# GpSimd computes two of the eight hidden units of every slot of a fused four-layer graph network

## The chip, the cores and the metric

The kernel runs on one core of one Trainium2 chip. The metric is the device time of one execution in microseconds, as the median of a few runs. The work is done by five engines with a program each: TensorE (PE in the profile, with its weight loads as PEld), VectorE (DVE), ScalarE (ACT), GpSimd (POOL) and SyncE (SP), which issues all DMAs here. The engines are tied together by semaphores that the code sets and waits on by hand.

## What is computed

For each of 64 graphs of 128 nodes with 128 features, four layers follow one another, each with a residual and a layer norm. The first is by far the largest:

```python
def _L0_gnn_ref(x, adj, W1, b1, W2, b2, gamma, beta):
    hi = jnp.einsum('bsh,hk->bsk', x, W1[:H])
    hj = jnp.einsum('bsh,hk->bsk', x, W1[H:])
    h = jax.nn.relu(hi[:, :, None, :] + hj[:, None, :, :] + b1)
    y = jnp.einsum('bijk,kl->bijl', h, W2) + b2
    y = _layernorm(y, gamma, beta)
    return jnp.einsum('bij,bijh->bih', adj, y)
...
x = _layernorm(x + _L0_gnn_ref(x, adj, ...), axis=-1)
x = _layernorm(x + _L1_gnn_ref(x, adj, W, b), axis=-1)      # relu((D^-1/2 adj D^-1/2 x) W^T + b)
x = _layernorm(x + _L2_gnn_ref(x, adj, nodemask, ...), axis=-1)   # two-layer perceptron on (1+eps)x + adj^T x
x = _layernorm(x + _L3_gnn_ref(x, adj, ...), axis=-1)      # three rounds of adj^T (h W), norm, relu
```

So for every graph and every node i there is a 128x128 block h_i = relu(v + u_i), where v (hj, turned so that features lie on the partitions) is the same for all i and u_i (hi + b1) is one column. All in float32.

## The kernel before

**Units, slots, graphs.** The 128x128 block of one node i is a unit. Eight units (`DUO_UNITS`) make a slot, in two blocks of four (`BLOCK_UNITS`); a graph has 16 slots (`SLOTS`). Every engine walks through the same sequence of slots s = 0..15 per iteration, and works in slot s on a different stage of an earlier slot t, at a fixed lag (`lagging`). Between its own steps of the first layer each engine has the steps of the three later layers of an older graph ("tails", placed by the table `AT`: slot and one of nine fine places k, `FINE`). In what follows "slot s" is a place in an engine's program, and t the slot of h that is treated there.

**The stages of one slot t.**
- Hidden, lag 4 (`START`): the eight units h = relu(vT + u_i) are made. VectorE makes the first `vector_units(t)` units from vT in SBUF with one tensor_scalar each (L624), two in a slot and four in slot 15: 34 of a graph. ScalarE makes the others, with one activation each that reads v from PSUM (L515, 90 of a graph) or, in slot 15, vT from SBUF (4 of a graph). The `h` buffer holds 16 slots, so that a slot of h can be written only when its weighted sums for the graph before are done (`ttr_done`).
- Products, lag 5: TensorE multiplies each block of four units with W2 into `y_ps` (L377; a float32 product is two instructions in the trace). Block 0 waits for `h_dve` and `h_act_head`, block 1 for `h_act`.
- Squares, lag 6: ScalarE squares the 128x1024 result into `sq` (L525). In its program this stands at the start of each slot, before the hidden units.
- Variances: TensorE sums the squares over the partitions (L389, eight instructions for every two slots). After half a graph ScalarE takes the root (L532), DMAs straighten it, VectorE takes the reciprocal (L646) and multiplies with adj (L654), and DMAs store and spread the coefficients over all partitions (`cb`).
- Weighted sums, lags 18 and 19: VectorE multiplies each unit of h with its row of coefficients and sums (L638, 128 of a graph: a custom instruction that reads h and cb, both in SBUF, and an accumulator read). In slot s it first does units 4 to 7 of one t (fine places 0 to 3), then at place 4 its hidden units, then units 0 to 3 of the next t (places 5 to 8).

At slot 3 TensorE makes u and v of the new graph and ScalarE copies them out (`keep_uv`, L504 and L505, which sets `uv_ready`).

GpSimd has only small steps on 128x1 columns: for each of the seven norms of a graph an addition (L865) and a power -1/2 (L868), and one more power (L860). VectorE needs the power six fine places after the statistics (`NORM_AT`).

The names that the change touches are `vector_units`, ScalarE's `hidden` and the loop that calls it, `keep_uv`, TensorE's `products`, and GpSimd's `iteration`.

Of the kernel before, what the change touches and what calls it, by code (L numbers as in the profile page):

```python
# [12 lines left out]
P = 128  # L13
# [20 lines left out]

NORM_AT = 7
LATER_SET_UP_SLOT = 2


def vector_units(t):

    if t == SLOTS - 1:
        return BLOCK_UNITS
    return 2

# [30 lines left out]
def build(nc, x, adj, nodemask, l0_W1, l0_b1, l0_W2, l0_b2, l0_gamma, l0_beta, l1_W, l1_b,  # L75
# [4 lines left out]
    with ExitStack() as ctx:  # L80
# [6 lines left out]
        def sem(name):  # L87
            return ctx.enter_context(nc.semaphore(name))
# [81 lines left out]
            sem("x_in_in"), sem("x_turned"), sem("xT_set"), sem("uv_made"), sem("uv_ready"))  # L170
        h_dve, h_act_head, h_act = sem("h_dve"), sem("h_act_head"), sem("h_act")
        y_done, sq_done = sem("y_done"), sem("sq_done")
# [178 lines left out]
        def _(pe):  # L351
# [15 lines left out]
            def products(g, t, block_of_duo):  # L367
# [6 lines left out]
                else:  # L374
                    wait(pe, h_act, SLOTS * g + t + 1)
                c0 = block_of_duo * COLS
                op = pe.matmul(y_ps[:, t % 2, c0:c0 + COLS], w2c[:], h[:, t, c0:c0 + COLS], start=True, stop=True)  # L377
# [115 lines left out]
        def _(act):  # L493
# [5 lines left out]
            def keep_uv(g, b):  # L499

                wait(act, uv_made, g + 1)
                wait(act, h_dve, SLOTS * (g - 1))
                wait(act, h_act, SLOTS * (g - 1))
                act.activation(uT[:, b, :], u_ps, ACT.Identity, bias=b1_col[:])  # L504
                act.activation(vT[:, b, :], v_ps, ACT.Copy).then_inc(uv_ready, 1)  # L505

            def hidden(g, b, t, n):
# [8 lines left out]
                if n == BLOCK_UNITS - 1:  # L516
                    op.then_inc(h_act_head, 1)
                if n == DUO_UNITS - 1:
                    op.then_inc(h_act, 1)
# [56 lines left out]
            def iteration(after, graphs, buf):  # L576
                new = graphs[0]
                for s in range(SLOTS):
# [17 lines left out]
                    first = vector_units(ht)  # L596
                    for n in range(first, DUO_UNITS):
                        if n == first + 2:
# [5 lines left out]
                        if hg is not None:  # L604
                            hidden(hg, hb, ht, n)
                    if first == BLOCK_UNITS:
                        tail_steps(6, 8)
# [219 lines left out]
        def _(pool):  # L827
# [26 lines left out]
            def later_layers(g, b, lo, hi):  # L854
# [7 lines left out]
                for name in NORMS:  # L862
                    if lo <= AT[name] + 1 < hi:
# [5 lines left out]
                                           ).then_inc(rs_set[name], 1)  # L869

            pool.wait_ge(ones_set, 5)

            def iteration(after, graphs, buf):
                for s in range(SLOTS):
                    for k in range(FINE):
                        for g, b, place in tails(graphs, buf, s):
                            later_layers(g, b, place + k, place + k + 1)
# [26 lines left out]
```

## Time and profile before

| | us |
|---|---|
| median of three runs (2913.82 to 2915.78) | 2914.24 |
| the profiled execution | 2916.74 |
| its span, first to last instruction | 2915.1 |
| PE busy | 2819.0 (97%) |
| ACT busy | 2824.1 (97%) |
| DVE busy | 2732.0 (94%) |
| POOL busy | 436.3 (15%) |
| mean granted TensorE clock | 0.99 |

Busy time is the time in which at least one instruction of the engine is under way. Instructions of one engine overlap (the next starts before the last has written its result), so the duration of an instruction is not what it costs: that is the distance from its start to the start of the next one when nothing is waited for. Both are used below, and named apart.

### The profile page before, as it was taken

To read this page: it belongs to the slowest core of one execution; us is meant where nothing else is said; L and a number is where in the kernel's file an instruction comes from. 1 tells how busy PE (TensorE), PEld (TensorE's weight loads), DVE (VectorE), ACT (ScalarE), POOL (GpSimd) and SP (SyncE) were. 2 spreads that over 40 slices of the span, in tenths; PEclk is the share of its full clock that TensorE was granted. 3 is DMA by queue.
4 is the path that set the end of the run, shared out by engine and by line. 5 is a ranking of instruction groups with operands and counts; after the bars stand their busy time and mean duration, and the time that the engine had idled before them with its cause. 6 is when DMAs were issued, how large, how long until landed. Compare 5 with 4: busy or idle time off the path is not lost.

```text
span 2915.1 us, 59519 instructions
## 1 busy us (share of the span) xinstructions
PE 2819.0 (97%) x10882; PEld 1093.6 (38%) x10882; DVE 2732.0 (94%) x21521; ACT 2824.1 (97%) x8004; POOL 436.3 (15%) x978
## 2 busy tenths in 40 slices
PE   8999999999999999999999999999999999999994
PEld 2333333333333333333333333333333333333332
DVE  3999999999999999999999999999999999999997
ACT  8999999999999999999999999999999999999992
POOL 0011111111111111111111111111111111111111
PEclk9999999999999999999999999999999999999996
DMA  2544544554555455445545544554554455455442
GB/s 101 225 185 191 223 196 183 212 214 184 194 217 199 185 205 221 185 191 217 203 182 212 213 185 190 221 199 185 208 218 186 185 226 199 183 209 217 185 191 114
DMA packets 170229, 571.63 MB, mean 196 GB/s; under 512 B 68608, under 2 KB 104320, under 8 KB 104320
## 3 DMA queue, kind: packets, MB, share of 16 engines
q1 hardware_dynamic: 169856, 567.82, 49.6%
q14 instruction: 282, 2.31, 0.2%
q8 instruction: 91, 1.49, 0.2%
HBM read 555.17 MB, written 8.39 MB: 193 GB/s over the span
## 4 chain that ended last, share of the span: by engine, by line
ACT 61%; PE 22%; issue 10%; DVE 4%; DMA 2%; SPq 1%; POOL 0%; DVEq 0%; POOLq 0%; ACTq 0%
ACT h L515 36%; ACT sq L525 16%; PE y_ps L377 14%; PE ss_ps L389 4%; ACT dev_rows L532 4%; DVE h L638 2%; ACT xT L497 2%; ACT hid L554 1%; DMA cb<-c_scratch 1%; PE uv_ps L364 1%; PE prod_bank L410 1%; ACT aggT L550 1%; DMA devs<-dev_rows 1%; SPq L294 1%; ACT aggT L558 1%
## 5 line engine op out<-in xcount | busy, mean ns | idle before, releaser
L377 PE MATMUL y_ps<-h,w2c 128*128 128x512 f32 x4096 | 2104.5, 621 | 32.9 <-issue 14.1
L515 ACT ACTIVATE h<-uv_ps,uT 128x128 f32<-128x128 f32 x5760 | 2011.9, 788 | 0.0
L638 DVE CUSTOM_DVE_ANT_0 h<-h,cb 128x128 f32<-128x128 f32 x8192 | 1923.1, 279 | 44.9 <-DMA cb<-c_scratch 42.6
L525 ACT ACTIVATE sq<-y_ps,b2c_col 128x1024 f32<-128x1024 f32 x1024 | 1550.9, 1515 | 24.5 <-PE y_ps L377 24.5
L377 PEld LDWEIGHTS y_ps<-h,w2c 128*128 128x128 f32 x4096 | 647.8, 189 | 1058.4 <-issue 691.6
L638 DVE DVE_READ_ACCUMULATOR2_ANT gT<- 128x1 f32 x8192 | 633.4, 77 | 0.0
L389 PE MATMUL ss_ps<-sq,sel 128*32 128x512 f32 x4096 | 546.4, 605 | 1.1 <-ACT sq L525 1.0
L624 DVE TENSOR_SCALAR h<-vT,uT 128x128 f32<-128x128 f32 x2176 | 501.1, 273 | 6.8 <-ACT mask_all L570 4.8
L865 POOL TENSOR_TENSOR var_eps<-mv,eps_col 128x1 f32<-128x1 f32 x448 | 85.7, 191 | 2004.1 <-DVE mv L665 2004.1
L868 POOL TENSOR_TENSOR rs<-var_eps,minus_half 128x1 f32<-128x1 f32 x448 | 308.5, 689 | 35.0
L389 PEld LDWEIGHTS ss_ps<-sq,sel 128*32 128x32 f32 x4096 | 80.6, 108 | 248.7 <-ACT sq L525 182.7
L646 DVE RECIPROCAL invs<-devs 128x64 f32<-128x64 f32 x128 | 70.6, 552 | 103.6 <-DMA devs<-dev_rows 103.2
L563 ACT ACTIVATE h<-z_aff 128x128 f32<-128x128 f32 x192 | 130.6, 680 | 18.7 <-DVE z_aff L745 18.7
L558 ACT ACTIVATE aggT<-prod_bank 128x128 f32<-128x128 f32 x192 | 128.2, 668 | 20.9 <-PE prod_bank L439 20.9
L515 ACT ACTIVATE h<-vT,uT 128x128 f32<-128x128 f32 x256 | 140.0, 914 | 0.0
L662 DVE BATCH_NORM_STATS2 stats<-z 128x6 f32<-128x128 f32 x448 | 127.0, 283 | 0.3
L532 ACT ACTIVATE dev_rows<-ss_ps 128x512 f32<-128x512 f32 x128 | 116.3, 909 | 1.0 <-PE ss_ps L389 1.0
L443 PEld LDWEIGHTS prod_bank<-l3w,aggT 128*128 128x128 f32 x384 | 68.3, 192 | 126.2 <-ACT aggT L558 89.4
L860 POOL TENSOR_TENSOR dis_raw<-degree_floor,minus_half 128x1 f32<-128x1 f32 x64 | 35.3, 551 | 416.0 <-DVE degree_floor L686 416.0
L443 PE MATMUL prod_bank<-l3w,aggT 128*128 128x128 f32 x384 | 82.7, 298 | 14.4 <-ACT aggT L558 14.2
L671 DVE TENSOR_SCALAR x<-z,mv,rs 128x128 f32<-128x128 f32 x256 | 86.4, 338 | 5.1 <-POOL rs L868 4.8
L665 DVE BATCH_NORM_AGGREGATE mv<-stats 128x2 f32<-128x6 f32 x448 | 76.6, 171 | 0.4
(99 smaller groups left out, 1592.9 us busy)
## 6 DMA issues: line engine op xcount, KB each, us to landing
cb<-c_scratch SPq DMA_DIRECT2D x512, 1024.0 KB, 8.2
adj_c<-in_adj_dram SPq DMA_DIRECT2D x512, 8.0 KB
devs<-dev_rows SPq DMA_DIRECT2D x512, 8.0 KB
x_in<-in_x_dram SPq DMA_DIRECT2D x64, 64.0 KB, 10.6
c_scratch<-c SPq DMA_DIRECT2D x128, 32.0 KB, 1.4
adj_in<-in_adj_dram SPq DMA_DIRECT2D x64, 64.0 KB, 4.3
x_res<-in_x_dram SPq DMA_DIRECT2D x64, 64.0 KB, 5.3
out_dram<-x SPq DMA_DIRECT2D x64, 64.0 KB, 3.0
```

Of the source, the lines that this page charges most:

```text
L377: op = pe.matmul(y_ps[:, t % 2, c0:c0 + COLS], w2c[:], h[:, t, c0:c0 + COLS], start=True, stop=True)
L389: mm = pe.matmul(ss_ps[32 * q:32 * q + 32, :], sel[:, ROWS - 1 - p:ROWS - 1 - p + 32], sq[:, (t + q // 2) % SQ_RING, c0:c0 + COLS], start= ...
L443: pe.matmul(out, aggT[:, b, :], l3w[:, i, :], start=True, stop=False)
L515: op = act.activation(h[:, t, n * P:(n + 1) * P], v, ACT.Relu, bias=uT[:, b, i:i + 1])
L525: act.activation(sq[:, t % SQ_RING, :], y_ps[:, t % 2, :], ACT.Square, bias=b2c_col[:], scale=float(P) ** -0.5).then_inc(sq_done, 1)
L532: act.activation(dev_rows[:, half, :], ss_ps[:], ACT.Sqrt, bias=EPS).then_inc(dev_done, 1)
L558: act.activation(aggT[:, b, :], prod[b], ACT.Copy).then_inc(l3_agg_kept[i], 1)
L563: act.activation(h3[:, b, :], z_aff[:, b, :], ACT.Relu).then_inc(l3_relued[i], 1)
L624: op = dve.tensor_scalar(h[:, t, n * P:(n + 1) * P], vT[:, b, :], uT[:, b, i:i + 1], 0.0, ALU.add, ALU.max)
L638: op = dve.tensor_tensor_reduce(h[:, t, cols], h[:, t, cols], cb[:, t // 2, c0:c0 + P], 1.0, 0.0, ALU.mult, ALU.add, gT[:, i:i + 1])
L662: dve.bn_stats(stats[:, b, :], z[:, b, :]).then_inc(stats_set[name], 1)
L868: pool.tensor_tensor(rs[:, b:b + 1], var_eps[:, b:b + 1], minus_half[:], ALU.pow).then_inc(rs_set[name], 1)
```

## The change

GpSimd gets two of the eight units of every slot, 32 of a graph: the last unit (7), at fine place 0 of the slot in which the other engines make theirs, and the unit before it (6), at fine place 6 of the slot ahead of that. It makes them from vT and uT with the same tensor_scalar as VectorE. Both wait for the weighted sums that read the old content of this slot of h, and in t = 0 for uv_ready. VectorE makes one unit in place of two (still four in slot 15): 19 of a graph. ScalarE makes units 1 to 5, and in slot 15 units 4 and 5: 77 of a graph. `h_pool` is a new semaphore, for which block 1 of the products waits, and `keep_uv`. The steps of the later layers keep their places; where ScalarE's loop has become too short for one of them, it comes after the loop.

```diff
@@ -33,14 +33,23 @@
 FINE = 1 + DUO_UNITS
 
 NORM_AT = 7
+EARLY_AT = 6
 LATER_SET_UP_SLOT = 2
 
 
 def vector_units(t):
 
-    if t == SLOTS - 1:
-        return BLOCK_UNITS
-    return 2
+    return BLOCK_UNITS if t == SLOTS - 1 else 1
+
+
+def early_unit(t):
+
+    return True
+
+
+def act_end(t):
+
+    return DUO_UNITS - (2 if early_unit(t) else 1)
 
 
 def unit_of(t, n):
@@ -168,7 +177,7 @@
 
         x_in_in, x_turned, xT_set, uv_made, uv_ready = (
             sem("x_in_in"), sem("x_turned"), sem("xT_set"), sem("uv_made"), sem("uv_ready"))
-        h_dve, h_act_head, h_act = sem("h_dve"), sem("h_act_head"), sem("h_act")
+        h_dve, h_pool, h_act_head, h_act = sem("h_dve"), sem("h_pool"), sem("h_act_head"), sem("h_act")
         y_done, sq_done = sem("y_done"), sem("sq_done")
         ttr_done = sem("ttr_done")
         var_summed = sem("var_summed")
@@ -373,6 +382,7 @@
                     wait(pe, sq_done, SLOTS * g + t - 1)
                 else:
                     wait(pe, h_act, SLOTS * g + t + 1)
+                    wait(pe, h_pool, SLOTS * g + t + 1)
                 c0 = block_of_duo * COLS
                 op = pe.matmul(y_ps[:, t % 2, c0:c0 + COLS], w2c[:], h[:, t, c0:c0 + COLS], start=True, stop=True)
                 if block_of_duo == 1:
@@ -501,6 +511,7 @@
                 wait(act, uv_made, g + 1)
                 wait(act, h_dve, SLOTS * (g - 1))
                 wait(act, h_act, SLOTS * (g - 1))
+                wait(act, h_pool, SLOTS * (g - 1))
                 act.activation(uT[:, b, :], u_ps, ACT.Identity, bias=b1_col[:])
                 act.activation(vT[:, b, :], v_ps, ACT.Copy).then_inc(uv_ready, 1)
 
@@ -515,7 +526,7 @@
                 op = act.activation(h[:, t, n * P:(n + 1) * P], v, ACT.Relu, bias=uT[:, b, i:i + 1])
                 if n == BLOCK_UNITS - 1:
                     op.then_inc(h_act_head, 1)
-                if n == DUO_UNITS - 1:
+                if n == act_end(t) - 1:
                     op.then_inc(h_act, 1)
 
             def squares(g, t):
@@ -594,7 +605,7 @@
                         deviations(vg, t // HALF)
                     tail_steps(1, 4)
                     first = vector_units(ht)
-                    for n in range(first, DUO_UNITS):
+                    for n in range(first, act_end(ht)):
                         if n == first + 2:
                             tail_steps(4, 6)
                         if n == first + 4:
@@ -603,7 +614,11 @@
                             keep_uv(new, buf)
                         if hg is not None:
                             hidden(hg, hb, ht, n)
-                    if first == BLOCK_UNITS:
+                    if act_end(ht) <= first + 2:
+                        tail_steps(4, 6)
+                        if s == START - 1 and new is not None:
+                            keep_uv(new, buf)
+                    if act_end(ht) <= first + 4:
                         tail_steps(6, 8)
                     if s == 12 and after is not None:
                         keep_xT(after, 1 - buf)
@@ -868,11 +883,29 @@
                         pool.tensor_tensor(rs[:, b:b + 1], var_eps[:, b:b + 1], minus_half[:], ALU.pow
                                            ).then_inc(rs_set[name], 1)
 
+            def hidden(g, b, t, n):
+
+                wait(pool, ttr_done, SLOTS * (g - 1) + t + 1)
+                if t == 0:
+                    wait(pool, uv_ready, g + 1)
+                i = unit_of(t, n)
+                op = pool.tensor_scalar(h[:, t, n * P:(n + 1) * P], vT[:, b, :], uT[:, b, i:i + 1], 0.0, ALU.add, ALU.max)
+                if n == DUO_UNITS - 1:
+                    op.then_inc(h_pool, 1)
+
             pool.wait_ge(ones_set, 5)
 
             def iteration(after, graphs, buf):
                 for s in range(SLOTS):
+                    hg, ht = lagging(graphs, s, START)
+                    hb = buf if s >= START else 1 - buf
+                    eg, et = lagging(graphs, s, START - 1)
+                    eb = buf if s >= START - 1 else 1 - buf
                     for k in range(FINE):
+                        if k == 0 and hg is not None:
+                            hidden(hg, hb, ht, DUO_UNITS - 1)
+                        if k == EARLY_AT and eg is not None and early_unit(et):
+                            hidden(eg, eb, et, DUO_UNITS - 2)
                         for g, b, place in tails(graphs, buf, s):
                             later_layers(g, b, place + k, place + k + 1)
```

The order of the instructions, at three places. A row of ScalarE, VectorE or GpSimd is one instruction (or several alike, "x4") with its line, its operation and out<-in; what it waits for stands in brackets.

First ScalarE, where one graph passes into the next: slots 2 and 3 of an iteration. Before (L515 hidden units, L525 squares, L504 and L505 keep_uv, L558 a step of the tail):

```order
L525 ACTIVATE sq<-y_ps,b2c_col 128x1024 [waits var_summed,y_done]
L515 ACTIVATE h<-uv_ps,uT 128x128 [waits ttr_done]
L515 ACTIVATE h<-uv_ps,uT 128x128 x5
L525 ACTIVATE sq<-y_ps,b2c_col 128x1024 [waits var_summed,y_done]
L515 ACTIVATE h<-vT,uT 128x128 [waits ttr_done]
L515 ACTIVATE h<-vT,uT 128x128
L504 ACTIVATE uT<-uv_ps,b_col 128x128 [waits h_act,h_dve,uv_made]
L505 ACTIVATE vT<-uv_ps 128x128
L515 ACTIVATE h<-vT,uT 128x128 x2
L558 ACTIVATE aggT<-prod_bank 128x128 [waits l3_agged1]
```

The same place of the changed kernel (L526 hidden units, L536 squares, L515 and L516 keep_uv, L569 the tail):

```order
L536 ACTIVATE sq<-y_ps,b2c_col 128x1024 [waits var_summed,y_done]
L526 ACTIVATE h<-uv_ps,uT 128x128 [waits ttr_done]
L526 ACTIVATE h<-uv_ps,uT 128x128 x4
L536 ACTIVATE sq<-y_ps,b2c_col 128x1024 [waits var_summed,y_done]
L526 ACTIVATE h<-vT,uT 128x128 [waits ttr_done]
L526 ACTIVATE h<-vT,uT 128x128
L515 ACTIVATE uT<-uv_ps,b_col 128x128 [waits h_act,h_pool,h_dve,uv_made]
L516 ACTIVATE vT<-uv_ps 128x128
L569 ACTIVATE aggT<-prod_bank 128x128 [waits l3_agged1]
```

An ordinary slot has one hidden unit fewer, slot 15's has two fewer, and nothing else has moved.

Second GpSimd, where the hidden units of a new graph begin. Before (L865 and L868, the two steps of the norm that the last word names):

```order
L860 TENSOR_TENSOR dis_raw<-degree_floor,minus_half 128x1 [waits dis_set,degree_floor_set]
L865 TENSOR_TENSOR var_eps<-mv,eps_col 128x1 [waits mv_set_ln0]
L868 TENSOR_TENSOR rs<-var_eps,minus_half 128x1 [waits eps_added_ln0]
L865 TENSOR_TENSOR var_eps<-mv,eps_col 128x1 [waits mv_set_l3_ln1]
L868 TENSOR_TENSOR rs<-var_eps,minus_half 128x1 [waits eps_added_l3_ln1]
```

The same place of the changed kernel (L892 hidden units, L875, L880 and L883 the old steps):

```order
L875 TENSOR_TENSOR dis_raw<-degree_floor,minus_half 128x1 [waits dis_set,degree_floor_set]
L892 TENSOR_SCALAR h<-vT,uT 128x128 [waits ttr_done] x6
L892 TENSOR_SCALAR h<-vT,uT 128x128 [waits uv_ready,ttr_done]
L880 TENSOR_TENSOR var_eps<-mv,eps_col 128x1 [waits mv_set_ln0]
L883 TENSOR_TENSOR rs<-var_eps,minus_half 128x1 [waits eps_added_ln0]
L892 TENSOR_SCALAR h<-vT,uT 128x128 [waits uv_ready,ttr_done]
L892 TENSOR_SCALAR h<-vT,uT 128x128 [waits ttr_done] x2
L880 TENSOR_TENSOR var_eps<-mv,eps_col 128x1 [waits mv_set_l3_ln1]
L883 TENSOR_TENSOR rs<-var_eps,minus_half 128x1 [waits eps_added_l3_ln1]
```

Each hidden unit waits, and what stands behind a waiting one waits with it: at this place the norm ln0 stands behind the early unit of t = 0, which waits for uv_ready.

Third VectorE, around fine place 4 of slot 0. Before (L638 weighted sums with their accumulator reads, L624 hidden units, L686 a step of the tail):

```order
L638 ISA gT 128x1
L624 TENSOR_SCALAR h<-vT,uT 128x128 [waits ttr_done]
L624 TENSOR_SCALAR h<-vT,uT 128x128
L638 ISA h,gT<-h,cb 128x128 [waits cb_in7]
L638 ISA gT 128x1
L686 TENSOR_SCALAR degree_floor<-degree 128x1 [waits degree_set]
L638 ISA h,gT<-h,cb 128x128
```

The same place of the changed kernel (L653, L639, L701):

```order
L653 ISA gT 128x1
L639 TENSOR_SCALAR h<-vT,uT 128x128 [waits ttr_done]
L653 ISA h,gT<-h,cb 128x128 [waits cb_in7]
L653 ISA gT 128x1
L701 TENSOR_SCALAR degree_floor<-degree 128x1 [waits degree_set]
L653 ISA h,gT<-h,cb 128x128
```

One hidden unit is gone, and the weighted sums follow one unit earlier.

## Rows read from the trace of the kernel before

**Rows 1.** Window of ten graphs: length, busy us (instructions) by engine, clock.

```profile
1040.00:1483.70 443.70, 437.71 (x1704) 169.32 (x1700) 425.75 (x3362) 440.40 (x1252) 67.80 (x150) 1.00 0.51 201
```

**Rows 2.** Groups of that window: busy, mean ns | idle before.

```profile
L377 PE MATMUL y_ps<-h,w2c 128*128 128x512 f32 x640 | 328.9, 620 | 3.8 <-issue 2.5
...
L646 DVE RECIPROCAL invs<-devs 128x64 f32<-128x64 f32 x20 | 11.0, 551 | 11.5 <-DMA devs<-dev_rows 11.5
```

**Rows 3.** Timeline of ACT: start, length, line, out<-in, count.

```profile
1412.94 1.17 ACT L532 ACTIVATE dev_rows<-ss_ps 128x512 f32<-128x512 f32 x1
1413.41 2.25 ACT L515 ACTIVATE h<-uv_ps,uT 128x128 f32<-128x128 f32 x6
...
1419.61 1.01 ACT L543 ACTIVATE adjT<-prod_bank 128x128 f32<-128x128 f32 x1
1419.77 1.37 ACT L515 ACTIVATE h<-uv_ps,uT 128x128 f32<-128x128 f32 x2
1420.27 1.87 ACT L525 ACTIVATE sq<-y_ps,b2c_col 128x1024 f32<-128x1024 f32 x1
1421.27 2.42 ACT L515 ACTIVATE h<-uv_ps,uT 128x128 f32<-128x128 f32 x6
1422.77 1.93 ACT L525 ACTIVATE sq<-y_ps,b2c_col 128x1024 f32<-128x1024 f32 x1
...
1429.65 1.90 ACT L515 ACTIVATE h<-uv_ps,uT 128x128 f32<-128x128 f32 x6
1431.88 1.11 ACT L525 ACTIVATE sq<-y_ps,b2c_col 128x1024 f32<-128x1024 f32 x1 [0.33 <-PE y_ps L377]
```

**Rows 4.** Timeline of DVE, in the same columns.

```profile
1417.64 0.55 DVE L646 RECIPROCAL invs<-devs 128x64 f32<-128x64 f32 x1 [0.86 <-DMA devs<-dev_rows]
...
1419.85 0.15 DVE L686 TENSOR_SCALAR degree_floor<-degree 128x1 f32<-128x1 f32 x1
1419.91 0.28 DVE L638 CUSTOM_DVE_ANT_0 h<-h,cb 128x128 f32<-128x128 f32 x1
...
1423.89 0.48 DVE L624 TENSOR_SCALAR h<-vT,uT 128x128 f32<-128x128 f32 x2
1424.28 0.22 DVE L702 COPY gT_keep<-gT 128x128 f32<-128x128 f32 x1
```

**Rows 5.** Timeline of PE, in the same columns.

```profile
1416.77 1.07 PE L389 MATMUL ss_ps<-sq,sel 128*32 128x512 f32 x8
1417.76 1.12 PE L377 MATMUL y_ps<-h,w2c 128*128 128x512 f32 x2
...
1442.22 0.38 PE L427 MATMUL prod_bank<-adj_in,x 128*128 128x128 f32 x2
1442.44 0.39 PE L428 MATMUL prod_bank<-ident_eps,x 128*128 128x128 f32 x2
1442.66 1.88 PE L377 MATMUL y_ps<-h,w2c 128*128 128x512 f32 x4
```

**Rows 6.** Timeline of POOL at the start of the program.

```profile
1.24 0.29 POOL L831 TENSOR_SCALAR_AFFINE_SELECT ident<-ident 128x128 f32<-128x128 f32 x1 [0.24 <-POOL sel L829]
...
22.84 0.61 POOL L848 CAST bias_head<-bias_row 128x512 bf16<-128x512 f32 x1
23.53 1.16 POOL L851 TENSOR_TENSOR bias_rest<-bias_row,bias_head 128x512 f32<-128x512 f32 x1
```

**Rows 7.** Timeline of POOL and DVE around a power.

```profile
1444.16 0.19 POOL L865 TENSOR_TENSOR var_eps<-mv,eps_col 128x1 f32<-128x1 f32 x1 [5.12 <-DVE mv L665]
...
1444.43 0.69 POOL L868 TENSOR_TENSOR rs<-var_eps,minus_half 128x1 f32<-128x1 f32 x1
...
1444.63 0.28 DVE L638 CUSTOM_DVE_ANT_0 h<-h,cb 128x128 f32<-128x128 f32 x1
...
1444.84 0.28 DVE L638 CUSTOM_DVE_ANT_0 h<-h,cb 128x128 f32<-128x128 f32 x1
...
1445.06 0.28 DVE L638 CUSTOM_DVE_ANT_0 h<-h,cb 128x128 f32<-128x128 f32 x1
```

## The prediction

> **What bounds the kernel now.** I read the busy times per graph first. In the window of ten graphs a graph takes 443.7 / 10 = 44.37 us, and ACT is busy for 44.04 of it, PE for 43.77 and DVE for 42.58 [rows 1]. Three engines look full. But busy time hides waits behind the ends of earlier instructions, so I read next, in the timelines, how far one start lies from the next, and count.
>
> ScalarE: from the squares to the next instruction 1.00 us (1420.27 to 1421.27), six hidden units 1.50, so 0.25 each [rows 3]. A graph has 16 squares (16.0), 94 units (23.5), two roots at 0.47 (0.9), and 13 more steps, of which the copy at 1419.61 costs 0.16 [rows 3]; at 0.16 to 0.25 they make some 2.5. That is 42.9 of 44.37 us. ScalarE is the bound in nearly all slots. Of the 1.5 us that are left much lies where a graph begins: the six units from 1429.65 end their turn at 1431.15, and the squares start at 1431.88, having waited for y_ps [rows 3].
>
> VectorE: its instructions follow one another closely, so busy is nearly cost: 42.6 us, of which a hidden unit is 0.39 / 2 = 0.195 [rows 4]. Of its idle 1.8 us, 1.15 are the reciprocal's wait for the DMA that straightens the deviations [rows 2].
>
> TensorE: a products instruction costs (1.88 - 0.62) / 3 = 0.42 us, its own length being 0.62 [rows 2, 5], the eight variance instructions cost 0.99 together, one of the tail 0.11 [rows 5]. A graph has 170 instructions [rows 1]: 64 of products (27.2), 64 of variances (8 x 0.99 = 7.9), 42 of the tail (4.6), together 39.7. A weight load that starts only after a wait adds about 0.1 each time (the two products instructions behind the variances need 1.12 where 0.42 + 0.62 = 1.04 would do [rows 5]); for 10 to 20 of these I add 1 to 2 us. So TensorE needs 40.7 to 41.7 us, and the rest of its 43.8 is waiting for ScalarE.
>
> **The change part by part.**
>
> ScalarE loses 17 x 0.25 = 4.2 us of a graph and comes to **38.7 us**. All of it is on the path.
>
> VectorE loses 15 x 0.195 = 2.9 us and comes to 39.6 us busy. It is not the bound before, so this is room and not time, and it is used at once, below.
>
> TensorE loses nothing. It gets one more wait (`h_pool`), in front of block 1 of the products; behind it stand that block, the variances and the steps of the tail, and ScalarE's squares wait for it. When is h_pool set? Both units of a slot wait only for the weighted sums that VectorE ends at fine place 3 of the slot before the one in which it makes its own unit. The power and the addition hold GpSimd for 0.27 + 0.69 = 0.96 us [rows 7]. With the two units behind them they are done some 1.6 to 1.9 us later, while VectorE's own unit of the same slot comes a whole slot (2.6 us) after the sums and block 0 waits for that. So h_pool costs nothing; that cover would go if a unit took over 0.8 us.
>
> GpSimd gains 32 units. **The trace shows no tensor_scalar on GpSimd.** From below, its 128x128 select takes 0.29 us; from above, a two-input operation takes 1.16 for 512 columns, of which 0.19 remain for one column [rows 6, 7], so 0.19 + 0.97 / 4 = 0.43 for 128 is an estimate. A one-input cast of 512 takes 0.61 [rows 6], which puts 128 columns near 0.3. I take 0.3 and keep 0.43. Its load is then 32 x 0.3 to 0.43 + 7 x 0.96 + 0.6 = 17 to 21 us of 42, with 0.6 for the eighth power taken like the others: no bound. The norms' powers stand mostly in front of the units (the sums and the statistics come at the same fine place), and VectorE wants them six places, some 1.8 us, later; ln0, which stands behind the early unit of t = 0, can be a few tenths late, once in a graph: 0 to 0.3 us on VectorE, taken as 0.1.
>
> **What GpSimd's units do to VectorE** is the term that decides. VectorE's weighted sums read h and cb, both in SBUF, and are 128 x 0.21 = 27 us of its 44. If GpSimd's reads hold them up, VectorE pays. The nearest rows are the powers: during the 0.69 us from 1444.43, sums start at 1444.63, 1444.84 and 1445.06 and take 0.28, 0.21 apart as ever [rows 7]. So an instruction on GpSimd does not shut VectorE out for its whole length. But these read a single column, and say little of 128. From below the price is zero. From above it is a unit's whole 0.43. In between: a weighted sum streams 128 elements in about 0.13 of its 0.21 us (a one-column tensor_scalar stands 0.06 before the next instruction, one of 128 columns 0.195 [rows 4]), and 128 columns cost the cast 0.61 / 4 = 0.15 at most on GpSimd. If the two streams can't overlap, a sum is put off by 0.15 less the 0.08 in which it doesn't stream, 0.07, up to 0.15. The first unit of a pair falls partly under VectorE's own hidden unit, which has one input. I take 0.09 for each of the 32: **2.9 us**, and VectorE comes to 39.6 + 2.9 + 0.1 = 42.6 less what its waits for DMAs take up. Such a wait is idle time that turns into work when VectorE is late, and the room of 1.8 us is mostly that [rows 1, 2].
>
> The Trainium skill speaks against this change: by "SBUF — State Buffer", section "Who interferes with whom", a VectorE instruction with two SBUF inputs contends with a GpSimd instruction that reads SBUF, and the loser blocks for the whole of the other. The powers here read SBUF and block nothing for 0.69 us, so the trace does not bear out the "whole" for one column; for 128 columns no row tells. By that rule the time would be rival B's.
>
> **The sum.** ScalarE 38.7, TensorE 40.7 to 41.7, VectorE 40 to 42.6. The longest sets the graph, and the three don't mesh perfectly: before, 1.5 us came on top of ScalarE's 42.9, at the graph's start. That place gets milder, since ScalarE and VectorE both have room to catch up. From TensorE's middle, 41.2, plus 1.1 of this, and from VectorE's 42.6 less some waiting, I come to **42.4 us a graph**. 64 graphs x (44.37 - 42.4) = 126 us off; the start and the end, where the engines are not full, stay. Span 2915.1 - 126 = 2789, the profiled execution 2791; the median of before is 2.5 below its profiled execution, so 2788.
>
> **The rivals.**
>
> A. *No contention, TensorE alone is the bound.* The sums stay 0.21 apart, 41.2 us a graph and little on top: 64 x 3.2 = 203 us off, 2711. For it speaks that the powers disturb nothing; against it that TensorE's waits for its inputs have never been absent. Between A and the forecast lies all that has a price under 0.05 per unit.
>
> B. *VectorE becomes the bound through the shared reading of SBUF* (slower than before). Place: the weighted sums at fine places 5 to 8 and 0 to 3. Price: a unit's whole 0.3, for the 24 of 32 that don't fall under VectorE's own unit: 7.2 us, VectorE 46.8, 64 x 2.4 = 156 us more, 3070. It turns slower from (44.37 - 39.6) / 32 = 0.15 us a unit; at 0.19 it gives 39.6 + 6.1 = 45.7 and 2999. For it speaks that two of VectorE's inputs must come from somewhere at the same time as GpSimd's; against it the three sums under the power.
>
> C. *The contention costs, but less than it gives:* 0.10 to 0.14 us a unit, VectorE 42.8 to 44.1, 2815 to 2898.
>
> D. *The freed time goes to waits for DMAs.* VectorE's reciprocal waits until 1417.64 for deviations whose root started at 1412.94: 4.7 us [rows 3, 4] over two slots of now 5.3, and shorter slots don't shorten DMAs. VectorE could then be pushed behind by up to 0.4 us twice a graph; TensorE takes some of it up before it needs h_dve. 42.9 us a graph, 2820. It is inside C's time.
>
> That GpSimd's units come late and the change doesn't do what it says would need 0.8 us a unit; no row of a plain operation on 128 columns comes near.
>
> **How the numbers follow.** Forecast (2755 to 2812) 0.38; A with all faster than 2755 0.20; C with D 0.15; within 0.2% of before (5.8 us, about what a measurement of this kernel can tell from no change) 0.03; B 0.24, half of it below 2990. Faster 0.73, same 0.03, slower 0.24. The range goes from 2705, under A, to 2990, so that 0.12 of B and 0.04 below A are left out. The likeliest sign's own range is 2705 to 2898.
>
> **What would show it.** The distance between weighted sums during a GpSimd unit: 0.21 for A, about 0.3 once per unit for the forecast, 0.5 for B. GpSimd's unit at 0.3 to 0.4 us. ACT busy with squares 1.00 apart from their follower, and waiting for y_ps in most slots where it now waits in one of sixteen. PE with fewer waits for h L526. If VectorE waits for neither DMA and has no idle time, it is the bound. The forecast is wrong if a unit costs VectorE over 0.15 us, or if TensorE's need is under 40.

## The result and the profile after

The changed kernel takes **2820.68 us** (median of four runs, 2811.44 to 2829.14), beside 2915.01 for the kernel before: ratio **0.9675 [0.9644, 0.9706]**, 94 us less. I had said 2788, from 2705 to 2990. Sign and range held; a quarter of the forecast gain is missing. The profiled execution was the slowest of the four, 2829.14 with a span of 2827.5.

The page of the changed kernel has these busy times, and this chain of work that ended last, by engine and by line:

```profile
PE 2720.4 (96%) x10882; PEld 1133.2 (40%) x10882; DVE 2655.9 (94%) x20561; ACT 2582.0 (91%) x6916; POOL 2131.9 (75%) x3026
...
DVE 61%; DMA 26%; PE 7%; issue 3%; ACT 1%; SPq 1%; POOL 0%; DVEq 0%; POOLq 0%; ACTq 0%
DVE h L653 38%; DMA cb<-c_scratch 19%; DMA c_scratch<-c 6%; DVE h L639 5%; PE y_ps L387 5%; DVE stats L677 3%; DVE gT L653 3%; DVE x L686 3%; DVE mv L680 1%; DVE z_aff L760 1%; PE ss_ps L399 1%; DVE invs L661 1%; DVE z_aff L755 1%; DVE z L747 1%; DVE c L669 1%
```

The page of before had this chain by engine:

```profile
ACT 61%; PE 22%; issue 10%; DVE 4%; DMA 2%; SPq 1%; POOL 0%; DVEq 0%; POOLq 0%; ACTq 0%
```

VectorE and the transfers between its steps now set the end: 61% and 26%. ScalarE has left the chain. PE reads 96% busy and holds 7% of it, so busy time alone would have named the wrong engine.

Groups of the same page (lines have moved: L526 is L515 of before, L536 L525, L387 L377, L653 L638, L661 L646; L892 is new). The columns are busy us, mean ns | idle before, and what ended most of it:

```profile
L653 DVE CUSTOM_DVE_ANT_0 h<-h,cb 128x128 f32<-128x128 f32 x8192 | 1994.0, 288 | 91.8 <-DMA cb<-c_scratch 91.1
L892 POOL TENSOR_SCALAR h<-vT,uT 128x128 f32<-128x128 f32 x2048 | 1698.5, 843 | 174.9 <-ACT vT L516 105.7
...
L536 ACT ACTIVATE sq<-y_ps,b2c_col 128x1024 f32<-128x1024 f32 x1024 | 1191.2, 1163 | 169.1 <-PE y_ps L387 163.3
...
L661 DVE RECIPROCAL invs<-devs 128x64 f32<-128x64 f32 x128 | 69.5, 543 | 47.8 <-DMA devs<-dev_rows 47.7
```

A unit costs GpSimd 0.83 us (1698.5 / 2048), where I took 0.3. ScalarE waits 163 us for the products. VectorE waits 91 us for the broadcast coefficients, where the page of before had this row:

```profile
L638 DVE CUSTOM_DVE_ANT_0 h<-h,cb 128x128 f32<-128x128 f32 x8192 | 1923.1, 279 | 44.9 <-DMA cb<-c_scratch 42.6
```

The reciprocal's waits of [rows 2] are nearly gone: 44.5 of its 47.7 us are one wait at the start. The window of ten graphs, beside [rows 1]:

```profile
1040.00:1465.00 425.00, 418.37 (x1684) 174.48 (x1682) 409.89 (x3179) 398.83 (x1074) 329.72 (x466) 1.00 0.54 209
```

TensorE's granted clock is 1.00 as before. A graph has 20561 / 64 = 321 instructions of VectorE, so the window holds 9.9 graphs. The time from graph to graph (the first write of uT in one to that in the next, read from the trace) is called the period below. Its mean from the fourth graph on, when the pipeline is full, is 42.8 us, 1.6 less than before. The first one stands apart: 57.4, where before it took 44.3. The start of the program, POOL and then PE (start, length, [idle before <- what ended it]), shows why:

```profile
22.13 0.60 POOL L860 CAST bias_parts<-bias_row 32x512 bf16<-32x512 f32 x1 [19.88 <-DMA l3beta<-in_L_gnn_betas_dram]
...
27.28 0.60 POOL L860 CAST bias_parts<-bias_row 32x512 bf16<-32x512 f32 x1
27.98 3.48 POOL L892 TENSOR_SCALAR h<-vT,uT 128x128 f32<-128x128 f32 x5
```

```profile
12.27 2.04 PE L387 MATMUL y_ps<-h,w2c 128*128 128x512 f32 x2 [1.70 <-ACT h L526]
29.54 7.39 PE L387 MATMUL y_ps<-h,w2c 128*128 128x512 f32 x10 [15.23 <-POOL h L892]
```

GpSimd sets up the bias before its first unit, and that waits for the last weights. TensorE stands for 15.23 us. So the account in the profiled spans (2915.1 to 2827.5, 87.6 us): 13.1 us lost in the first graph, and 100 gained in the 62 periods behind it, whose mean falls from 44.31 to 42.70. I had forecast 64 x 1.97 = 126.

### The profile page after: what moved, and what is told of

Read it like the earlier page. It is cut to its first block, busy times and chain, and to the rows that moved or that the text cites. A ratio compares the mean times of both kernels' runs of the same rounds, so it can differ in the third digit from the quotient of the medians.

```text
span 2827.5 us, 60731 instructions
## 1 busy us (share of the span) xinstructions
PE 2720.4 (96%) x10882; PEld 1133.2 (40%) x10882; DVE 2655.9 (94%) x20561; ACT 2582.0 (91%) x6916; POOL 2131.9 (75%) x3026
## 4 chain that ended last, share of the span: by engine, by line
DVE 61%; DMA 26%; PE 7%; issue 3%; ACT 1%; SPq 1%; POOL 0%; DVEq 0%; POOLq 0%; ACTq 0%
DVE h L653 38%; DMA cb<-c_scratch 19%; DMA c_scratch<-c 6%; DVE h L639 5%; PE y_ps L387 5%; DVE stats L677 3%; DVE gT L653 3%; DVE x L686 3%; DVE mv L680 1%; DVE z_aff L760 1%; PE ss_ps L399 1%; DVE invs L661 1%; DVE z_aff L755 1%; DVE z L747 1%; DVE c L669 1%
## 5 line engine op out<-in xcount | busy, mean ns | idle before, releaser
L387 PE MATMUL y_ps<-h,w2c 128*128 128x512 f32 x4096 | 2041.9, 613 | 55.7 <-DVE h L639 35.5
L653 DVE CUSTOM_DVE_ANT_0 h<-h,cb 128x128 f32<-128x128 f32 x8192 | 1994.0, 288 | 91.8 <-DMA cb<-c_scratch 91.1
L892 POOL TENSOR_SCALAR h<-vT,uT 128x128 f32<-128x128 f32 x2048 | 1698.5, 843 | 174.9 <-ACT vT L516 105.7
L526 ACT ACTIVATE h<-uv_ps,uT 128x128 f32<-128x128 f32 x4800 | 1433.1, 440 | 4.5 <-DVE gT L653 4.4
L536 ACT ACTIVATE sq<-y_ps,b2c_col 128x1024 f32<-128x1024 f32 x1024 | 1191.2, 1163 | 169.1 <-PE y_ps L387 163.3
L387 PEld LDWEIGHTS y_ps<-h,w2c 128*128 128x128 f32 x4096 | 675.4, 190 | 996.1 <-issue 516.2
L653 DVE DVE_READ_ACCUMULATOR2_ANT gT<- 128x1 f32 x8192 | 629.0, 77 | 0.0
L880 POOL TENSOR_TENSOR var_eps<-mv,eps_col 128x1 f32<-128x1 f32 x448 | 94.6, 211 | 371.8 <-DVE mv L680 369.8
L639 DVE TENSOR_SCALAR h<-vT,uT 128x128 f32<-128x128 f32 x1216 | 338.6, 292 | 5.5 <-ACT mask_all L581 3.5
L883 POOL TENSOR_TENSOR rs<-var_eps,minus_half 128x1 f32<-128x1 f32 x448 | 301.8, 674 | 35.0
L661 DVE RECIPROCAL invs<-devs 128x64 f32<-128x64 f32 x128 | 69.5, 543 | 47.8 <-DMA devs<-dev_rows 47.7
L875 POOL TENSOR_TENSOR dis_raw<-degree_floor,minus_half 128x1 f32<-128x1 f32 x64 | 35.2, 550 | 90.2 <-DVE degree_floor L701 90.2
L686 DVE TENSOR_SCALAR x<-z,mv,rs 128x128 f32<-128x128 f32 x256 | 92.2, 360 | 5.1 <-POOL rs L883 4.8
L574 ACT ACTIVATE h<-z_aff 128x128 f32<-128x128 f32 x192 | 75.0, 391 | 19.7 <-DVE z_aff L760 19.7
L543 ACT ACTIVATE dev_rows<-ss_ps 128x512 f32<-128x512 f32 x128 | 81.2, 634 | 5.8 <-PE ss_ps L399 5.4
L569 ACT ACTIVATE aggT<-prod_bank 128x128 f32<-128x128 f32 x192 | 61.7, 321 | 20.7 <-PE prod_bank L449 20.7
```

What stands on the lines that cost most here:

```text
L526: op = act.activation(h[:, t, n * P:(n + 1) * P], v, ACT.Relu, bias=uT[:, b, i:i + 1])
L536: act.activation(sq[:, t % SQ_RING, :], y_ps[:, t % 2, :], ACT.Square, bias=b2c_col[:], scale=float(P) ** -0.5).then_inc(sq_done, 1)
L639: op = dve.tensor_scalar(h[:, t, n * P:(n + 1) * P], vT[:, b, :], uT[:, b, i:i + 1], 0.0, ALU.add, ALU.max)
L653: op = dve.tensor_tensor_reduce(h[:, t, cols], h[:, t, cols], cb[:, t // 2, c0:c0 + P], 1.0, 0.0, ALU.mult, ALU.add, gT[:, i:i + 1])
L686: dve.tensor_scalar(dst[:, b, :], z[:, b, :], mv[:, b, 0:1], rs[:, b:b + 1], ALU.subtract, ALU.mult).then_inc(normed[name], 1)
L883: pool.tensor_tensor(rs[:, b:b + 1], var_eps[:, b:b + 1], minus_half[:], ALU.pow).then_inc(rs_set[name], 1)
```

## The experiments

All ratios are to the kernel before, run on the same chip in between. The kernel before took 2915.01 us beside the changed kernel, and 2910.7, 2916.68 and 2916.11 in the three batches of experiments, so a difference of two times from different batches is known to some 5 us only. The ratios don't have this error. My theory after seeing the trace had three parts: the late start (theory S), VectorE as bound through contention with GpSimd's reads (K), and the coefficients' transfers, which VectorE now waits for (D, of the kind of rival D).

**Later bias.** GpSimd's bias set-up is cut in steps, done in slots 9 to 15 of the first graph behind its units:

```
+                        if k == 0 and is_graph(graphs[0], 0) and 0 <= s - 9 < 7:
+                            wait(pool, h_pool, SLOTS * hg + ht + 1)
+                            bias_step(s - 9)
```

> The changed kernel with GpSimd's seven set-up operations for the bias rows moved from ahead of its first hidden unit to slots 9 to 15 of the first graph, one in each. Theory S (the changed kernel starts late): its first hidden unit starts at 27.98 us because these operations wait for the last of the weights, TensorE waits 15.2 us for it, and the first graph takes 57.4 us where it took 44.3. Without that the first unit starts near 11 us, the first graph takes 41 to 44 us, and the time falls by 13 to 16 us, to about 2806. Rival: the late start is made good later, since the engines behind it then run without waits; the time stays near 2820.

Measured: 2812.43 us, 0.9661 [0.9646, 0.9676]. The first graph takes 40.9 us and not 57.4, and POOL and PE start so:

```profile
11.40 8.64 POOL L896 TENSOR_SCALAR h<-vT,uT 128x128 f32<-128x128 f32 x12 [9.15 <-ACT vT L516]
```

```profile
12.29 8.14 PE L387 MATMUL y_ps<-h,w2c 128*128 128x512 f32 x12 [1.69 <-DVE h L639]
```

The wait of 15 us is gone, so the late start is real. The median fell only 8.3 us, under the 13 to 16 expected, and the intervals of the two kernels overlap (by the ratios it is 4 us); the profiled spans, 2827.5 and 2807.7, differ by 20, of which 16 lie in the first graph. How much of the start is in the median is known no better than that from this pair. Twelve units in 8.64 us also give a unit's cost when VectorE is hardly in the way: 0.72.

**Units that read nothing.** GpSimd's units become writes alone, so their numbers are left out; all waits stay:

```
-                op = pool.tensor_scalar(h[:, t, n * P:(n + 1) * P], vT[:, b, :], uT[:, b, i:i + 1], 0.0, ALU.add, ALU.max)
+                op = pool.memset(h[:, t, n * P:(n + 1) * P], 0.5)
```

> The changed kernel with GpSimd's hidden units replaced by a memset of the same 128 columns: it writes SBUF and reads none (the numbers in these units are left out, so the output is not the reference's). Theory C (VectorE is the bound, and GpSimd's reads are part of its load): the weighted sums stand 0.21 apart again everywhere, VectorE's busy time falls by 1.7 us a graph to 39.6, and the time falls by 60 to 110 us, to 2710 to 2760. Rival P (TensorE and the meshing of the engines are the bound): VectorE's busy time falls, its idle time grows by as much, and the time stays at 2805 to 2825. Rival D (the DMAs of the coefficients are the bound): waits for cb grow by about what is saved, the time falls by 10 to 40 us.

Measured: 2782.15 us, 0.9555 [0.9541, 0.9569], 38.5 under the changed kernel (35 by the ratios). Its page:

```profile
PE 2702.7 (97%) x10882; PEld 1130.7 (41%) x10882; DVE 2542.1 (91%) x20561; ACT 2575.8 (93%) x6916; POOL 820.7 (29%) x3026
...
PE 72%; DVE 13%; DMA 9%; ACT 2%; issue 2%; SPq 2%; POOL 0%; DVEq 0%; POOLq 0%; ACTq 0%
...
L653 DVE CUSTOM_DVE_ANT_0 h<-h,cb 128x128 f32<-128x128 f32 x8192 | 1934.1, 283 | 138.5 <-DMA cb<-c_scratch 138.5
```

VectorE's 20561 instructions cost 2655.9 - 2542.1 = 113.8 us less: that is the contention, 0.056 us for each of 2048 units. What is left, 2542.1 / 64 = 39.7 us a graph, is about the 39.6 that I had without contention, so plain writes cost VectorE next to nothing. This run also makes the units shorter and GpSimd earlier, but the single instructions agree: of 966 weighted sums that started beside a memset none was followed by the next later than 0.26 us, and of 3043 beside a unit of the changed kernel 477 were. So writing alone puts nothing off; that it is the reading, and not something else of the longer instruction, is an inference. Of the 113.8 us only 38.5 reach the time: the wait for cb grows from 91 to 138.5, which is what rival D of this run's expectation said, and then TensorE is the bound.

**Spare units in the kernel before.** The other way round: the kernel before with its own division of labour, and GpSimd making two units a slot that nobody reads or waits for.

```
+                pool.tensor_scalar(spare[:, spares[0] % 4, :], ident[:], minus_half[:], 0.0, ALU.add, ALU.max).then_inc(spare_made, 1)
```

> The kernel before, with two more tensor_scalars of 128x128 on GpSimd in every slot, at the places of the change, that read constants in SBUF and write a spare tile; nobody waits for them, and nothing is taken off any engine. It prices a GpSimd unit by itself. Theory C: VectorE's weighted sums near a unit are put off, its busy time rises by about 0.05 us a unit, 1.7 a graph, from 42.6 to 44.3 of 44.4; ScalarE stays the bound, but VectorE's waits for DMAs no longer fit beside it: 2920 to 2960. No contention: 2915 and VectorE busy for 2732 us as before. GpSimd's unit stands 0.7 to 0.9 us from the next in both.

Measured: 2946.24 us, 1.0123 [1.0106, 1.014].

```profile
PE 2785.2 (95%) x10882; PEld 1128.8 (38%) x10882; DVE 2856.1 (97%) x21521; ACT 2828.7 (96%) x8004; POOL 2162.0 (73%) x3026
...
DVE 87%; DMA 6%; issue 3%; ACT 2%; PE 1%; DVEq 0%; POOL 0%; SPq 0%; POOLq 0%; ACTq 0%
...
L878 POOL TENSOR_SCALAR spare<-ident,minus_half 128x128 f32<-128x128 f32 x2048 | 1730.7, 857 | 171.1 <-DVE gT L640 155.1
```

GpSimd's units, which here take no work off anyone, make the kernel 36 us slower, and VectorE's share of the chain is 87%, where it was 4%. VectorE's busy time rises by 2856.1 - 2732.0 = 124 us, 0.061 for a unit. K stands: two independent edits give 0.056 and 0.061. Rival A in its plain form (no contention) is out, and so is B (0.15 and more).

**The coefficients' first transfer in two.** The first broadcast of each half (two slots of coefficients) is cut in two, and VectorE's first slot waits for the first piece alone:

```
+                    if p == 0:
+                        A = DUO_UNITS * P
+                        sp.dma_start(cb[:, CHUNKS * half, 0:A], src[0:A].partition_broadcast(P)).then_inc(cb_head[half], 16)
+                        sp.dma_start(cb[:, CHUNKS * half, A:2 * A], src[A:2 * A].partition_broadcast(P)
+                                     ).then_inc(cb_in[CHUNKS * half], 16)
+                        continue
...
-                    if t % 2 == 0:
+                    if t % HALF == 0:
+                        wait(dve, cb_head[t // HALF], 16 * (g + 1))
+                    elif t % 2 == 0 or t % HALF == 1:
```

> The changed kernel with the first of the four DMAs that spread the coefficients of a half graph cut in two, so that the weighted sums of its first slot wait for 512 KB instead of 1024 KB. Rival D (the DMA between the coefficients and the first weighted sum, 6.1 to 8 us, is on the path in the changed kernel): the wait of VectorE for cb falls from 91 us in all to under 40, and the time falls by 30 to 60 us, to 2760 to 2790. Theory C: VectorE's waits fall as well and some of it comes back elsewhere, 10 to 30 us. Rival P: time as the changed kernel, 2810 to 2830.

Measured: **2781.02 us, 0.9553 [0.9539, 0.9567]**, 40 under the changed kernel (36 by the ratios).

```profile
PE 2703.2 (97%) x10882; PEld 1130.5 (41%) x10882; DVE 2658.0 (96%) x20561; ACT 2568.2 (92%) x6916; POOL 2136.7 (77%) x3026
...
PE 74%; DVE 14%; DMA 6%; issue 2%; ACT 2%; SPq 2%; POOL 0%; DVEq 0%; POOLq 0%; ACTq 0%
...
L663 DVE CUSTOM_DVE_ANT_0 h<-h,cb 128x128 f32<-128x128 f32 x8192 | 1999.6, 289 | 27.6 <-DMA cb<-c_scratch 18.5
```

VectorE is as busy as before the split (2658.0), and the wait for cb falls from 91.1 to 18.5: by 0.57 us for each of 128 halves. The first transfer of a half lands 4.67 us after its issue in the changed kernel, and its first piece here after 4.01 (medians from the trace), which is about that. So the transfers, beside the contention, were what held the changed kernel. The chain of the changed kernel at such a place (start, length, what) reads:

```profile
1120.77 0.14 DVE c L669
...
1120.94 1.44 DMA c_scratch<-c
...
1122.40 4.76 DMA cb<-c_scratch
...
1127.18 0.29 DVE h L653
```

From the coefficient to the first weighted sum 6.4 us pass, more than two slots of some 2.65, and 6.2 of them are the two transfers.

**The same split in the kernel before**, as a control.

> The kernel before with the first coefficient DMA cut in two. VectorE waits 42.6 us for cb in the kernel before, and ScalarE is the bound there. Theory: the wait goes, VectorE is idle elsewhere instead, and the time stays within 5 us of before; what the same cut gives the changed kernel (40 us) is there because the bound has moved. Rival: the DMA was on the path before as well, 10 to 30 us faster.

Measured: 2914.79 us, 0.9992 [0.9983, 1.0002]: nothing, although the wait for cb fell here too (42.6 to 5.2). The wait for the deviations grew from 103 to 125.6 us, and ScalarE stays the bound with 63% of the chain:

```profile
L656 DVE RECIPROCAL invs<-devs 128x64 f32<-128x64 f32 x128 | 70.8, 553 | 125.8 <-DMA devs<-dev_rows 125.6
```

The transfers' 40 us are a cost only once ScalarE's 4.2 us a graph have been taken away.

**Both repairs, split and later bias**, in one kernel.

> The changed kernel with both mends: the first DMA of the coefficients cut in two, and GpSimd's set-up for the biases moved behind its first units. The mends take 40 and 8 us alone. If they lie at different places (start of the program, DMA in every graph) they add up: 2765 to 2777. If TensorE is the bound by now (it is idle for 0.11 us of a graph's 42.0 with the split alone), the start's part still shows, since it lies ahead of the steady state: the same range. Rival: over 2780, if the late start only moves where the first waits lie.

Measured: **2766.14 us (2763.77 to 2767.81), 0.9481 [0.9467, 0.9495]**. This is the best complete kernel of this study, 150 us under before and 55 under the change. Alone the repairs gave 40 and 8 in the medians, 47 and 20 in the profiled spans, where both together give 61: they add up as far as the spread of the changed kernel's own times (18 us) lets one say. The period is 42.05.

**Both repairs, and units that read nothing** (their numbers left out again):

> The same with GpSimd's hidden units replaced by memsets of the same columns, which read no SBUF (these units' numbers are left out, the output is not the reference's). VectorE's busy time falls from 41.4 to 39.6 us a graph. Theory P (once the DMA's wait is gone TensorE is the bound, and GpSimd's reads cost nothing more): within 10 us of the kernel with both mends. Theory C (VectorE is still the bound): 60 to 110 us below it.

Measured: 2759.77 us, 0.9459 [0.9445, 0.9473].

```profile
PE 2696.1 (98%) x10882; PEld 1128.7 (41%) x10882; DVE 2552.9 (93%) x20561; ACT 2566.8 (93%) x6916; POOL 816.8 (30%) x3026
...
PE 92%; DVE 2%; DMA 2%; ACT 2%; issue 1%; SPq 1%; POOL 0%; DVEq 0%; POOLq 0%; ACTq 0%
```

Without contention only 6 us more come off, and 92% of the chain is TensorE's. That measures TensorE's own need: a period of 41.9 us, in which it is idle for 0.07. I had 40.7 to 41.7.

**One unit on GpSimd instead of two.** Without the early unit (`early_unit` false) the gain should come from one side only. First with VectorE relieved, and then with ScalarE relieved (`vector_units` 2):

> Part of the change alone: GpSimd makes only the last unit of each slot, taken off VectorE (19 a graph, as in the change), and ScalarE keeps its six (93 a graph, one fewer). ScalarE's need stays at 42.9 - 0.25 = 42.6 us a graph. If ScalarE was the bound before, this gives next to nothing: 2895 to 2915. If what VectorE was late by counts as well, up to 1 us a graph more: 2840 to 2890.

Measured: 2934.16 us, 1.0057 [1.004, 1.0073], slower than before, where 2895 to 2915 was expected. The trace shows where: the median period is 44.4 as before, ScalarE is busy for 43.8 us of a graph where it was 44.0, and the first graph takes 59.1. It is the late start, 15 us of some 18, without any gain over it. I had forgotten my own theory S here.

> The other part alone: GpSimd makes only the last unit of each slot, taken off ScalarE (78 a graph), and VectorE keeps two (34 a graph). ScalarE's need falls to 42.9 - 4.0 = 38.9 us, VectorE's rises by 16 x 0.056 = 0.9 to 43.4 us, and with its waits for DMAs of up to 1.4 it is the bound: 43.8 to 44.8 a graph, 2875 to 2930. If VectorE were not the bound of the changed kernel but TensorE, about 42.5 a graph: 2800 to 2830.

Measured: 2920.8 us, 1.0012 [1.0003, 1.0021].

```profile
DVE 78%; DMA 17%; issue 2%; ACT 1%; SPq 1%; PE 0%; POOL 0%; DVEq 0%; POOLq 0%
```

ScalarE is free, and VectorE, with its old work and one unit's contention, takes its place at a period of 44.3. Both halves hold the late start too, but their periods, 44.4 and 44.3, show that without it each would be worth 0.1 us a graph at most. Only both together make a gain, because ScalarE and VectorE, at 44.04 and 42.58 us busy of a graph [rows 1], stood so near each other.

**The early unit in the other's slot.** Both units one behind the other, at the start of the slot, where the change puts one of them at its middle:

```
                         if k == 0 and hg is not None:
+                            hidden(hg, hb, ht, DUO_UNITS - 2)
                             hidden(hg, hb, ht, DUO_UNITS - 1)
-                        if k == EARLY_AT and eg is not None and early_unit(et):
-                            hidden(eg, eb, et, DUO_UNITS - 2)
```

> The changed kernel with GpSimd's early unit moved to fine place 0 of the slot in which the other engines make theirs, in front of the last unit. GpSimd needs 2 x 0.83 us of a slot of 2.6 and runs through its queue as its waits allow; only the steps of the norms now stand in front of the pair in place of between. Theory Q (GpSimd is late for nobody, so the place doesn't matter): 2810 to 2830. Rival L (being ahead is what makes two units possible): TensorE waits for h_pool in many slots, 0.2 us or more each, over 2850.

Measured: 2829.57 us, 0.9701 [0.9687, 0.9716]; the change's 0.9675 [0.9644, 0.9706] overlaps it. The medians differ by 9 us, the profiled spans by 0.5 and the periods by nothing (42.8 both), so no run shows that the place matters. A slot of 2.67 us has room for two units of 0.83 and a power at either place: TensorE waits for h_pool once, at the start, in both.

**Four units fewer on VectorE.** On top of both repairs, VectorE makes none in every fourth slot (15 of a graph, ScalarE 81), to see whether the division could be better still:

> The changed kernel with both mends, and VectorE's unit given to ScalarE in four of the sixteen slots (VectorE 15 of a graph, ScalarE 81, GpSimd 32). VectorE's busy time falls by 0.8 us a graph to 40.6, ScalarE's need rises by 1.0 to 39.7. Theory P (TensorE is the bound): within 5 us of 2766. Theory C (VectorE is the bound): 30 to 50 us faster.

Measured: 2795.52 us, 0.9581 [0.9565, 0.9597], 29 slower than with both repairs alone. Both theories missed.

```profile
L670 DVE CUSTOM_DVE_ANT_0 h<-h,cb 128x128 f32<-128x128 f32 x8192 | 1995.0, 289 | 44.2 <-DMA cb<-c_scratch 41.3
...
L678 DVE RECIPROCAL invs<-devs 128x64 f32<-128x64 f32 x128 | 70.6, 551 | 87.1 <-DMA devs<-dev_rows 86.6
```

VectorE's waits for transfers double (20.6 and 45.5 with both repairs), as if everything in front of them came later; TensorE's weight loads wait for ScalarE's units 190 times, 51.5 us in all, against 120 times and 33. A slot in which ScalarE makes one unit more may then be late by that unit's 0.25. That a slot's delay is not made good in the next would fit, but no run tells it from another cause: this stays open.

## Why the prediction was right or wrong, step by step

**ScalarE: right.** Its unit costs 0.25 us as before, its busy time fell by 3.8 us a graph (4.2 in the sum), and it is the bound no longer: it waits for y_ps 265 times, 66 before.

**GpSimd's unit: the term was mis-sized.** I took 0.3 with 0.43 as the upper bound; it is 0.83, and 0.69 to 0.72 at the start, where little runs beside it. The failed step is the scaling of a cast of 512 columns to 128 by the columns alone, and of a tensor_tensor in the same way: neither has a scalar read per partition and two operations, and a group with those was nowhere in the trace. GpSimd's load is 33 us of a graph and not 17 to 21, and still no bound. By "0.8 us a unit" the cover of h_pool should have gone. It hasn't: after the one wait of 15.2 at the start TensorE waits for h_pool no more. My rule for the cover was too strict, since VectorE's unit of the slot comes later than both anyway (TensorE's weight loads wait for that one 593 times), and the early unit is made in the slot before. Nor did the powers behind the units come late: VectorE's waits for them are 4.8 and 3.0 us in all, before and after, where I had put 0.1 us a graph.

**Contention: right in kind, mis-sized.** I took 0.09 us a unit, 2.9 a graph; it is 0.056, 1.8 a graph. The timeline of VectorE during GpSimd's units shows who pays:

```profile
1411.08 2.40 POOL L892 TENSOR_SCALAR h<-vT,uT 128x128 f32<-128x128 f32 x3
...
1411.25 0.38 DVE L686 TENSOR_SCALAR x<-z,mv,rs 128x128 f32<-128x128 f32 x1
1411.55 0.28 DVE L653 CUSTOM_DVE_ANT_0 h<-h,cb 128x128 f32<-128x128 f32 x1
...
1411.76 0.28 DVE L653 CUSTOM_DVE_ANT_0 h<-h,cb 128x128 f32<-128x128 f32 x1
...
1411.98 0.38 DVE L639 TENSOR_SCALAR h<-vT,uT 128x128 f32<-128x128 f32 x1
1412.28 0.28 DVE L653 CUSTOM_DVE_ANT_0 h<-h,cb 128x128 f32<-128x128 f32 x1
```

Most sums stay 0.21 apart. Of those that start beside a unit about one in six (477 of 3043) stands 0.30 from the next, and none over 0.37; of the others none is put off. This is what I said, "about 0.3 once per unit", by size, but less often: some one such sum for every four units. The hidden unit of VectorE, of which I wrote that it "has one input" and so would shelter GpSimd's, is held up itself: 0.30 to the next start, where [rows 4] have 0.195. Of the 113.8 us that units without reads give back to VectorE, 73 lie at the weighted sums and 25 at its hidden units (from each start to the next, added up by line). So I had the main sharer right, its price too high, and the second sharer at nothing.

The Trainium skill ("SBUF — State Buffer", section "Who interferes with whom") lets a VectorE instruction with two SBUF inputs contend with a GpSimd instruction that reads SBUF, and spares GpSimd's plain writes; both edits above agree (units that read cost, the writes of memset cost next to nothing). The same section of the Trainium skill has the loser blocked for the whole of the other. Here the measurement differs and decides: of a unit's 0.83 us a hit costs 0.09 to 0.11. The Trainium skill also says in that section that a one-input tensor_scalar can contend where it runs in a mode with both ports, and L639 and L686 do contend; outside a hit it gives 128 columns in 0.13 us [rows 4], and no row shows whether they run in that mode.

**VectorE's waits: the step that failed.** "42.6 less what its waits for DMAs take up. Such a wait is idle time that turns into work when VectorE is late." That holds for the deviations, whose waits nearly vanished. For the coefficients it is the other way round: the chain is from VectorE's own coefficients through two transfers back to VectorE, so that a late VectorE starts the transfers late too, and shorter slots leave less cover: 42.6 became 91.1. The other runs agree: the wait is 17.2 where spare units made the period 44.9, and 138.5 where writes alone made it 42.1. Rival D had the right mechanism at the wrong transfer. That its time, 2820, is the measured one is partly luck: its 42.9 us a graph came out, but it had no late start in it. The split gives 36 to 40 us, more than the 26 by which the graphs missed my 42.4; with both repairs and the contention of 1.8 us left in, the period is 42.05.

**TensorE's need: right within 0.2.** 41.9 measured, 41.7 the upper end.

**"The start and the end stay": wrong for the start.** I had the casts of GpSimd's start in [rows 6], at 22.84 and 23.53, and used them only for their length. Hidden units now stood behind them in the queue. It cost 13 us in the first graph; with the 26 of the graphs that is the 38 us by which the profiled span misses my 126 (the median misses it by 32).

So the two misses that made it slower (start, coefficients' transfers) were partly paid by a contention smaller than I took, 1.8 us a graph and not 2.9. That the time came out within 33 us of the forecast owes something to this luck.

## What to carry to other kernels

When the bound engine is relieved, look at every loop in which the next engine waits for a transfer of its own result: such a wait does not turn into work, it grows as the slots shrink, and splitting the first transfer can be worth nearly half the change, though it is worth nothing before the relief. When work is given to an idle engine, read what stands at the start of its queue, and measure one of its instructions in the very form rather than scale it from another. And where two engines stand within a few per cent of each other, a relief of either alone may give nothing, as here.

## What the runs showed of the hardware

GpSimd takes 0.69 to 0.72 us for a tensor_scalar of 128x128 f32 with a scalar per partition and two operations when little runs beside it, 0.83 beside a busy VectorE; a memset of the same size is 0.22 long. If the difference is what it pays for VectorE's reads, which no run here isolates, GpSimd pays about 0.12 for a unit, twice what VectorE does (0.056 to 0.061). A one-input tensor_scalar on VectorE is put off beside GpSimd's units as well as a two-input sum: 0.11 us for the one, 0.09 for the other, where it is hit at all. And in the changed kernel no weighted sum is over 0.37 us from the next, beside GpSimd instructions of 0.71 to 1.13. A broadcast of 1 MB from DRAM has its first use 4.5 to 4.9 us after its issue in most of the chain's rows, and two halves of it, the first awaited alone, take four fifths of VectorE's wait away here (91.1 to 18.5 us).
